# A first attention layer rebuilt in row strips, with the next group's dense products inside the last batch

## What is computed

```python
x = x + tanh(g_xattn[0]) * L0_xattn(layernorm(x), ctx_512, Wq, Wkv_expand, Wout)

def L0_xattn(q, latent_kv, Wq, Wkv_expand, Wout):   # 16 heads of 16
    qp = q @ Wq.T
    k, v = split(latent_kv @ Wkv_expand.T, 2, axis=-1)
    scores = einsum('bhqd,bhkd->bhqk', heads(qp), heads(k)) / sqrt(16)
    scores = where(causal, scores, finfo.min)
    attn = softmax(scores, axis=-1)
    return einsum('bhqk,bhkd->bhqd', attn, heads(v)) @ Wout.T
```

## Time and profile before

| | |
|---|---|
| median of 3 runs | 3306.21 us |
| profiled execution, its own time | 3314.55 us |
| its span, first to last instruction | 3312.8 us |
| mean granted TensorE clock, of full | 0.929 |
| TensorE busy, whole span | 2855.9 us (86%) |
| VectorE busy, whole span | 2276.1 us (69%) |
| first attention, 42.9 to 436 us | 393.1 us; TensorE busy 370.7, VectorE 297.4, scalar engine 130.4 |
| granted clock in that stretch | 0.87 |

### The profile page before, as it was taken

How to read it: one execution, slowest core, us unless ns; L and a number is a source line. 1 busy time by engine, 2 the same in 40 slices (tenths; PEclk the granted TensorE clock), 3 DMA queues, 4 the chain that set the end, 5 groups by cost and what they waited for, 6 DMA issues and landing times. The chain is left out here.

```text
span 3312.8 us, 62826 instructions
## 1 busy us (share of the span) xinstructions
PE 2855.9 (86%) x18352; PEld 1925.8 (58%) x18352; DVE 2276.1 (69%) x4050; ACT 1658.2 (50%) x3458; POOL 1749.6 (53%) x1268
## 2 busy tenths in 40 slices
PE   5999979999799899898998999899989989996335
PEld 4777769999655565565555555556556556553123
DVE  5778764444376676677677667767767667666887
ACT  1333322222147646647646655654764664663556
POOL 0000012322167757667666666766765766763566
PEclk9888879999899999999999999999999999998566
DMA  4000010000201100000100000010110100011100
GB/s 112 0 0 0 0 48 10 5 10 10 75 6 25 22 12 21 19 16 17 23 18 17 21 18 17 16 26 7 24 22 11 22 19 16 11 50 35 42 13 25
DMA packets 130259, 71.17 MB, mean 21 GB/s; under 512 B 83582, under 2 KB 124510, under 8 KB 129880
## 3 DMA queue, kind: packets, MB, share of 16 engines
q1 hardware_dynamic: 129944, 67.45, 8.2%
HBM read 56.95 MB, written 10.04 MB: 20 GB/s over the span
## 5 line engine op out<-in xcount | busy, mean ns | idle before, releaser
L1200 POOL TENSOR_TENSOR c_psum<-c_p 120x800 f32<-120x800 f32 (+1 forms) x384 | 758.4, 1980 | 454.3 <-ACT c_p L1514 199.8
L1514 ACT ACTIVATE c_p<-c_s_ps 120x400 f32<-120x400 f32 (+1 forms) x1536 | 650.9, 513 | 301.7 <-PE c_s_ps L1686 231.3
L1698 PE MATMUL c_o_ps<-c_p,c_val 120*64 120x400 f32 (+1 forms) x3072 | 614.8, 523 | 10.9 <-ACT c_onum L1479 10.9
L1279 DVE TENSOR_REDUCE c_mpart<-c_m_ps 128x1 f32<-128x484 f32 x416 | 271.4, 652 | 204.3 <-PE c_m_ps L1593 204.2
L1324 DVE TENSOR_TENSOR c_acc<-c_acc,c_psum 120x800 f32<-120x800 f32 x256 | 370.2, 1446 | 59.9 <-POOL c_psum L1200 57.9
L1593 PE MATMUL c_m_ps<-c_kmax,c_q 64*128 64x484 f32 x1080 | 308.4, 438 | 90.6 <-DVE c_mpart L1279 49.1
L1191 POOL TENSOR_TENSOR l_rr<-c_psum,l_rr 96x400 f32<-96x400 f32 x256 | 264.2, 1053 | 190.5 <-DVE l_rr L1346 190.4
L1698 PEld LDWEIGHTS c_o_ps<-c_p,c_val 120*64 120x64 f32 (+1 forms) x3072 | 191.5, 139 | 281.1 <-issue 163.5
L1682 PE MATMUL c_s_ps<-c_q,c_k 64*120 64x400 f32 (+1 forms) x1536 | 321.4, 370 | 1.7 <-ACT c_p L1514 1.7
L1285 DVE CUSTOM_DVE_ANT_0 c_xt<-c_m_ps,c_xt,c_mpart 128x484 fp32r<-128x484 f32 x360 | 259.8, 722 | 86.5 <-DVE c_mpart L1279 45.4
L1629 PE MATMUL c_s_ps<-c_xt,l_a 128*96 128x400 f32 x1536 | 310.4, 352 | 9.8 <-DVE l_rr L1346 8.0
(11 more groups left out here) (259 smaller groups left out, 5304.6 us busy)
## 6 DMA issues: line engine op xcount, KB each, us to landing
c_rdb<-l_denominators SPq DMA_DIRECT2D x128, 100.0 KB, 2.7
c_kv<-in_ctx SPq DMA_DIRECT2D x32, 360.0 KB
c_mrow<-c_mneg SPq DMA_DIRECT2D x288, 0.5 KB, 2.0
x_rows<-in_x SPq DMA_DIRECT2D x4, 800.0 KB
x_spill<-x_rows SPq DMA_DIRECT2D x8, 400.0 KB
l_xa<-x_spill SPq DMA_DIRECT2D x8, 400.0 KB
c_xr<-x_spill SPq DMA_DIRECT2D x32, 100.0 KB
x_spill<-c_xr SPq DMA_DIRECT2D x32, 100.0 KB
```

What stands on the lines that cost most here:

```text
L1200: g.tensor_tensor(psum[0:k, u % 2, :], p[0:k, 2 * u % 4, :], p[0:k, (2 * u + 1) % 4, :], ALU.add).then_inc(psum_ready, 1)
L1279: v.tensor_reduce(mpart[:, t:t + 1], m_ps[:, bank, 0:4 * KP], AX.X, ALU.max, negate=True).then_inc(mpart_ready, 1)
L1514: a.activation(p[0:k, w % 4, i * HALFQ:(i + 1) * HALFQ], s_ps[0:k, (2 * w + i) % 4, 0:HALFQ], ACT.Exp).then_inc(exp_ready, 1)
L1698: mm = pe.matmul(o_ps[i * DL:(i + 1) * DL, 0:HALFQ], val[0:k, j % 2, r, :], p[0:k, w % 4, i * HALFQ:(i + 1) * HALFQ], start=(r == 0), stop ...
```

## The change

Sixteen heads are split otherwise. A quarter q now is a strip of 32 rows: heads 2q and 2q+1 of each half. Queries and keys stay where the dense products put them. A key operand `kbd` for a half holds two copies of the group's keys, one with the odd heads cleared and one with the even ones (`parity`), written straight from PSUM: half 0 by the scalar engine, half 1 by VectorE. The scores of one batch are eight 32-row products of 200 columns (L407), two for each bank; they all start only when all four banks have been masked again, which each does after its difference of the batch before. The order of dense pieces is new (latents, rows, keys, queries, values), the first four go into the last batch's banks as they come free, values and one key half are evacuated by the scalar engine. `keep_busy` (L354) is a product whose result is overwritten: 256 float32 columns through an identity. It stands in front of masks 1 and 2, transposes 0 and 1, and dense pieces 4 to 8.

```diff
-        headsel_raw, headsel = sb("a_headsel_raw", [128, 8]), sb("a_headsel", [128, 8, S])
+        parity = sb("a_parity", [128, 2])
-        kbd = [sb(f"a_kbd{i}", [128, KT, 8, S]) for i in range(2)]
+        kbd = sb("a_kbd", [128, KT, 2, T])
...
+        LATENTS, ROWS0, ROWS1, KEYS0, KEYS1, QUERIES0, VALUES0, VALUES1, QUERIES1 = range(9)
         ND = 9
+        FILL_MASKS, FILL_TURNS = (1, 2), (0, 1)
+        VEC_OUT = (LATENTS, ROWS0, ROWS1, KEYS1, QUERIES0, QUERIES1)
+        ACT_OUT = (KEYS0, VALUES0, VALUES1)
...
+                    elif n == KEYS1:
+                        for e in range(2):
+                            ins = v.tensor_scalar(kbd[:, 1, e, :], src, parity[:, e:e + 1], None, ALU.mult)
...
-                def block_keys(it, b):
...
                     for b in range(G):
                         for q in range(NQ):
...
+                            differences(b, q)
+                            if b == G - 1 and more and q < 3:
+                                evacuate(it + 1, (LATENTS, ROWS0, ROWS1)[q])
+                            if q == 1 and b > 0:
+                                normalise(b - 1)
+                            if q == 1 and b > 1:
+                                add_x(b - 2)
+                        if b == 0 and more:
+                            row_stats(it + 1)
+                        if b == 1 and more:
+                            normalise_rows(it + 1)
                     if more:
...
+                        evacuate(it + 1, KEYS1)
+                        evacuate(it + 1, QUERIES0)
+                    else:
+                        split_moe()
+                    add_x(G - 2)
+                    normalise(G - 1)
+                    if more:
+                        evacuate(it + 1, QUERIES1)
                     add_x(G - 1)
...
+                def keep_busy(bank):
+                    pe.matmul(bank[0:S, 0:D], m.ident[0:S, 0:S], lat[:, 0:D], start=True, stop=True)
...
+                def scores(it, b):
+                    pe.wait_ge(mask_done, PRIMED + (it * G + b + 1) * NQ)
+                    pe.sem_inc(m.carrier, 1)
+                    for k in range(KT):
+                        for q in range(NQ):
+                            rows = slice(32 * q, 32 * (q + 1))
+                            mm = pe.matmul(s_ps[0:S, q, 2 * k * S:2 * (k + 1) * S], qt[rows, k, b * S:(b + 1) * S],
+                                           kbd[rows, k, :, b * S:(b + 1) * S], start=False, stop=True, skip_group_check=True)
+                            if k == KT - 1:
+                                mm.then_inc(s_ready, 1)
...
+                    def next_bank(b, q):
+                        if b + 1 < G:
+                            pe.wait_ge(diff_ready, PRIMED + (it * G + b) * NQ + q + 1)
+                            if q in FILL_MASKS:
+                                keep_busy(s_ps[:, q, :])
+                            place_mask(q)
+                        elif more:
+                            dense(it + 1, q)
                     for b in range(G):
...
+                        next_bank(b, 0)
+                        turn_probs(b, 0)
+                        next_bank(b, 1)
+                        turn_probs(b, 1)
+                        probs_value(b, 0)
+                        next_bank(b, 2)
+                        next_bank(b, 3)
+                        if b + 1 < G:
+                            scores(it, b + 1)
+                        elif more:
+                            dense(it + 1, KEYS1)
+                        turn_probs(b, 2)
+                        probs_value(b, 1)
+                        if b > 0:
+                            turn_out(b - 1)
+                        turn_probs(b, 3)
+                        probs_value(b, 2)
+                        if b == G - 1 and more:
+                            dense(it + 1, QUERIES0)
+                        if b > 0:
+                            project_out(b - 1)
+                        if b == G - 1 and more:
+                            dense(it + 1, VALUES0)
+                        probs_value(b, 3)
                     if more:
...
+                        dense(it + 1, VALUES1)
                     turn_out(G - 1)
+                    if more:
+                        dense(it + 1, QUERIES1)
                     project_out(G - 1)
+                    if more:
+                        first_scores(it + 1)
```

More of the change, by code:

```diff
@@ L295, in _ @@
                 normalise_rows(0)
-                for k in range(ND):
+                for k in VEC_OUT:
                     evacuate(0, k)
-                v.wait_ge(dense_out, PRIMED + 7)
-                block_keys(0, 0)
                 v.wait_ge(x_rest, 16 * 3)
@@ L306, in _, with evacuate, group @@
             def _(a):
-                with a.Fori(0, NG) as it:
+                def evacuate(it, n):
+                    a.wait_ge(dense_mm, PRIMED + it * ND + n + 1)
+                    a.sem_inc(m.carrier, 1)
+                    if n == KEYS0:
+                        for e in range(2):
+                            ins = a.activation(kbd[:, 0, e, :], s_ps[:, n % 4, 0:T], ACT.Copy, scale=parity[:, e:e + 1])
+                    else:
+                        for j in range(2):
+                            ins = a.activation(va[:, 2 * (n - VALUES0) + j, :, 0:HD],
+                                               s_ps[0:S, n % 4, j * D:(j + 1) * D].rearrange("p (h d) -> p h d", h=H), ACT.Copy)
+                    ins.then_inc(act_out, 1)
+                def group(it, more):
                     def copy_ct(b):
@@ L324, in _ @@
                             a.activation(prob[:, q], diff[:, q], ACT.Exp, scale=HD ** -0.5).then_inc(prob_ready, 1)
+                            if q == 3 and b == G - 1 and more:
+                                evacuate(it + 1, KEYS0)
                             if q > 0:
-                                copy_pt(q - 1)
-                            if q == 1 and b > 0:
-                                copy_ct(b - 1)
-                        copy_pt(NQ - 1)
-                    copy_ct(G - 1)
+                                copy_pt(b, q - 1)
+                        if b > 0:
+                            copy_ct(b - 1)
+                        copy_pt(b, NQ - 1)
+                    if more:
+                        evacuate(it + 1, VALUES0)
+                    copy_ct(G - 1)
+                    if more:
+                        evacuate(it + 1, VALUES1)
+                for k in ACT_OUT:
+                    evacuate(0, k)
+                with a.Fori(0, NG - 1) as it:
+                    group(it, True)
+                group(NG - 1, False)
             @block.tensor
@@ new lines, in probs_value @@
+                    def probs_value(b, q):
+                        nb = it * G + b
+                        pe.wait_ge(pt_copied, PRIMED + nb * NQ + q + 1)
+                        if q == 0:
+                            pe.wait_ge(cn_ready, PRIMED + nb)
+                            pe.wait_ge(act_out, PRIMED + (it + 1) * len(ACT_OUT))
+                        for i, h in enumerate(heads(q)):
+                            mm = pe.matmul(o_ps[0:S, h * (HD + 1):(h + 1) * (HD + 1)], pt[:, q % 2, i, :], va[:, b, h, :], start=True, stop=True)
+                        mm.then_inc(pv_done, 1)
@@ L438, in group @@
                     if more:
-                        for k in range(7, ND):
-                            dense(it + 1, k)
+                        dense(it + 1, VALUES1)
                     turn_out(G - 1)
+                    if more:
+                        dense(it + 1, QUERIES1)
                     project_out(G - 1)
+                    if more:
+                        first_scores(it + 1)
                 for k in range(ND):
                     dense(0, k)
+                first_scores(0)
```

199 lines of the change are left out of this document (78 added, 121 removed).

## The result

The changed kernel takes 3360.95 us (median of 4 runs, 3359.99 to 3364.06); the kernel before, run beside it, 3306.04 us. The ratio is 1.0167, 95% interval 1.0155 to 1.018: 54.9 us slower. The forecast was 3409 us in a range of 3325 to 3480.

A forecast was written before the change was run, and what follows sets the result against it. Groups were taken as bound by TensorE's length, VectorE where it feeds it, and the lost clock. 3314.55 + 43 (dense part at half) + 60 (low batches) = 3417.6; the median being 8.3 lower, 3409 us, range 3325 to 3480.

The forecast's parts named there:

- rival A: First layer's attention: fills hold the clock in the batches, only the dense part is at half; about 3345 us, chance 0.30.
- B: The forecast's own case: some or all groups low in the batches, +70 to +166, 3376 to 3472 us; chance 0.45.
- Gaps of the batches: First reductions of batches 0 to 3 in a group: 6.5, 7.8 and 8.9 us apart at full clock.
- The last part: Batch 3 to the next group: 27.5 us at full clock against 30.9, with three TensorE idle times.
- Clock in the dense part: Clock falls in every group's last batch; 13.3 us at half cost 6.7, group 57.4 us, +43 us over seven periods.
- +60 us for low batches: Batches 1, 2 and early 3 at half clock: +17.5 us per group, taken for half of the seven groups.
- C: Clock stays full even in the last batch: -10 us, 3296 us; chance 0.10.
- D: Score strips don't run side by side: 2.0 us more per batch, 64 in all, 3414 to 3480 us; chance 0.10.
- E: No change: gains and clock cancel, 3300 to 3312 us; chance 0.05.
- the old order at full clock: A group of the kernel before at full clock would be near 44.5 us, shorter than the new order's 50.7.
- 1.8 us a batch on scores: Score products side by side in fours: gain of 1.8 us per batch, 7.2 per group.
- the 9 us of VectorE a group: Near 9 us of work leaves VectorE, but buys little since TensorE's length decides in batches 1 to 3.

The follow-up runs named there:

- 15 fills more: Changed kernel plus 15 filling products (4, 5 and 6) in TensorE's three idle times of the last batch; 3371.5 us, ratio 1.0186 to 1.0224.
- three fills: Kernel before plus only three filling products in TensorE's idle time ahead of the first query product; 3290.3 us, ratio 0.9942 to 0.997.
- normalisation first: Changed kernel with all four last-batch differences first, then batch 2's normalisation, then the latents' and rows' splits; runs of 3277, 3277, 3363, 3372 us.
- differences first: Changed kernel with VectorE taking all four last-batch differences before the splits of latents and rows; 3321.2 us, ratio 1.0026 to 1.0117.
- no dense fills, normalisation first: Changed kernel with last-batch differences, then batch 2's normalisation, ahead of the splits, and without the dense part's five filling products; 3289.1 us.
- no dense fills: Changed kernel without the five filling products of the dense part; 3362.0 us, ratio 1.0157 to 1.022.
- fills by batch: Changed kernel with last-batch differences, then normalisation, ahead of the splits, and 14 filling products a group placed by batch instead of 19; 3312.2 us.

## Why the prediction was right and where it was wrong

The measured 3361 us lie in the range because the range was wide enough for two stories. What happened is the less likely one, rival A. The forecast's own case (B, 3409 us) did not occur.

**Gaps of the batches: right.** 6.5, 7.8, 8.9 at full clock were forecast, 6.5, 7.9, 8.8 came in six of seven groups (the first has 8.0, 7.9, 8.8). One reason was incomplete: for batch 0 to 1 the forecast let VectorE's row statistics decide and gave TensorE room. In the last group, which has no statistics, the gap is 6.5 as well, VectorE stands 2.05 us, as long as they take elsewhere, and TensorE, once released by the first difference (1.23 us of idle time), works without a break up to the scores. Timeline, VectorE, changed kernel:

```profile
458.06 0.57 DVE L231 TENSOR_TENSOR a_diff<-a_s_ps,a_mx 100x400 f32<-100x400 f32 x1
460.68 0.57 DVE L227 TENSOR_REDUCE a_mx<-a_s_ps 100x4 f32<-100x400 f32 x1 [2.05 <-PE a_s_ps L407]
```

Both ends meet, so moving the statistics alone would win nothing (not tried).

**The last part: right.** 27.5 at full clock was the sum, and 34.7 less 7.2 is 27.5. The three idle times were forecast as 1.8, 2.1 and 2.6 us; the trace has 1.66, then 1.17 and 0.18 together, then 2.45. VectorE's stand ahead of the latents' split is 3.15 (forecast 1.2 to 4.4).

**Clock in the dense part: right mechanism, term slightly small.** It fell in each group, behind the first two idle times and ahead of the third, so that the 2.45 us stand in the stretch at half. 13.3 us at half and 6.7 lost were taken over from the earlier trace rows; it was 17.1 us with 14.47 of work in it, 7.2 lost. So 57.9 a group instead of 57.4, and 46.2 us over the seven periods for the forecast's 43. The start took 3.4 us more and the last group 2.1 less, for the 0 taken for both. Of the remaining 7.5 us of the 54.9, 5.4 are the difference between the two profiled runs (49.5 us apart) and the medians; 2.1 lie outside this phase.

**The failing step is the +60 us for low batches in half of the groups.** None of seven was low in batches 1 and 2, and only the first had a short fall in batch 0; rival A, at 3345 us with a chance of 0.30, is what happened, 16 us low. What the forecast called a batch at half is real: without fills every group shows it, and with 15 fills more two of seven show 11.4 and 16.6. The forecast named what decided, that the fills bring the streaming back to about that of the old batches, and then gave it half the weight. The runs with and without the 14 fills of the batches show that they carry the clock there: 0 us in place of +60. The forecast's bounds (0 and +122) held the truth at one end; the middle was a mean, not a case. The error shows as only 48 us, since 12 us came in elsewhere: 3.2 in the dense part, 1.3 at start and end, and the 7.5 above.

**Rivals C, D and E.** D is excluded by 0.87 a batch, E by 54.9 us. C's clock did not stay. The forecast's claim that the old order at full clock is the shorter (44.5 us) is confirmed in part by three fills: 47.9 with 6.8 at half, which is 44.5 if half of that goes. The new order without the wait chain comes to 45.2 at full clock (normalisation first): about level.

**Where the expected gain went.** 1.8 us a batch on scores were real, and so was most of the 9 us of VectorE a group: 38.9 became 30.6 us, 8.3 less. The first was spent on fills, and without those of the batches the clock falls. The second was worth little in the batches, and the new place of the splits turned VectorE into the bound of the last batch, where its in-order queue put each difference behind a wait for TensorE: 6.6 us a group by the run with differences first, 4.5 of it length and 2.1 clock.

## What to carry to other kernels

Where a granted clock can fall, streaming less is not a gain by itself: count what TensorE still does in each stretch, and look at the clock of that stretch first. An in-order engine that alternates between a critical chain and work that waits for another engine makes both wait; finish the chain's short pieces first. The cheapest fix here was three filling products in an idle time that was there anyway (0.4% faster, every run alike); the variants of the longer rebuild had better single runs (3270 us), but none of them had all its runs below the kernel before.

## What the hardware showed that was not expected

- The same instructions ran at either level. One program (no dense fills, normalisation first) shows groups of 44 us and of 65 to 73 us, and a low clock lasted 48 to 65 us through stretches which, in other groups of the same program, ran at full.
- TensorE was busy 95% of 82 us at half level (one strip of 32 rows at a time). Its busy time alone was no sign of the clock.
- The second layer's groups take 263 to 267 us in most kernels (the first of them up to 270), but mostly 268 to 270 us in three (no dense fills; normalisation first without them; fills by batch) with the same code. In the first of these, just behind a group's first score products, the clock falls where TensorE stands for 1.66 us. Columns as in the earlier trace rows:

```profile
1790.00:1797.00 7.00, 6.31 (x31) 3.74 (x29) 5.97 (x10) 3.90 (x8) 4.85 (x5) 1.00 0.03 5
1797.00:1804.00 7.00, 4.63 (x22) 2.85 (x24) 0.40 (x1) 2.86 (x6) 0.54 (x2) 0.67 0.16 39
```

  In the changed kernel the same place keeps 1.00:

```profile
1818.00:1825.00 7.00, 6.33 (x47) 3.55 (x46) 1.07 (x3) 5.91 (x12) 3.25 (x3) 1.00 0.14 36
```

  That is up to 7 us a group, some 22 in all. Why these kernels and not the others stays open; a change of this size in one phase has to be read in that phase.
- Swapping the order of the eight products changed nothing, although each second one then has the rows of the one ahead of it. Of the 16 records of a batch there, four start within 44 ns (230.047 to 230.091) and the next at 230.268, as in the changed kernel (four within 20 ns, the next 0.20 us later). With two products in a row on the same strip that fits only if a product for a free strip starts ahead of one that waits for its rows.
